# Handing out the scatter of the edges in ones and twos per step, and the rest beside the first layer norm

## What is computed

```
edge_index = stack([src, dst])
x = x + L0_gnn(layernorm(x), src, dst, edge_weight)     # segment_sum(w * x[dst], src), then a projection
x = x + L0_ffn(layernorm(x))                            # 16 experts, 2 per token
x = x + L1_gnn(layernorm(x), src, dst, edge_weight)
x = x + L1_ffn(layernorm(x))
x = x + L2_gnn(layernorm(x), src, dst)                  # graph attention, two layers
x = x + L2_ffn(layernorm(x))
x = x + L3_gnn(layernorm(x), edge_index, edge_weight)   # three rounds of segment sums
x = x + L3_ffn(layernorm(x))
```

## Time and profile before

| | |
|---|---|
| median of 3 runs | 6410.36 us |
| lowest, highest | 6409.36, 6415.48 us |
| span of the profiled execution (its own time; the page gives none around it) | 7555.1 us |
| PE busy in it | 5066.7 us, 67% |
| DVE busy | 2842.8 us, 38% |
| POOL busy | 2221.8 us, 29% |
| bin table's columns (L382) | 392, 402.3 us busy, mean 1026 ns |

### The profile page before, as it was taken

One profiled execution on the slowest core, in us unless ns is written; L12 is line 12 of the kernel. 1 busy time (PEld: TensorE's weight loads), 2 busy tenths in 40 slices (PEclk: granted clock), 3 DMA queues, 4 the chain that ended last, 5 costly groups with the idle time before them and its releaser, 6 DMA issues. The chain is left out here.

```text
span 7555.1 us, 86117 instructions
## 1 busy us (share of the span) xinstructions
PE 5066.7 (67%) x21628; PEld 3356.8 (44%) x21677; DVE 2842.8 (38%) x6162; ACT 1117.7 (15%) x2691; POOL 2221.8 (29%) x2417
## 2 busy tenths in 40 slices
PE   3511969659783597755454965554877969898954
PEld 2410547314771256733222843222767844444433
DVE  4260679201323004244445944445943220202052
ACT  2210235000220002210000120000123220101020
POOL 3356010540244401425553215553300410000014
PEclk9999999769796697977776976777988989999966
DMA  0000023223561223637774827675721644243323
GB/s 14 1 1 1 1 93 139 81 66 120 160 199 65 77 90 123 195 122 228 219 218 137 273 86 224 216 222 160 254 67 40 191 153 153 101 139 115 115 69 114
DMA packets 484296, 952.76 MB, mean 126 GB/s; under 512 B 112617, under 2 KB 292436, under 8 KB 481686
## 3 DMA queue, kind: packets, MB, share of 16 engines
q1 hardware_dynamic: 324614, 633.98, 24.9%
q0 software_dynamic: 114208, 281.05, 12.8%
q10 hardware_dynamic: 45296, 35.56, 1.6%
HBM read 733.91 MB, written 216.46 MB: 126 GB/s over the span
## 5 line engine op out<-in xcount | busy, mean ns | idle before, releaser
L1173 PE MATMUL banks<-ring,xn 128*128 128x512 f32 (+1 forms) x3500 | 1443.9, 568 | 397.6 <-issue 276.9
L1173 PEld LDWEIGHTS banks<-ring,xn 128*128 128x128 f32 x3500 | 644.2, 195 | 1198.0 <-issue 1181.4
L1909 PE MATMUL banks<-agg,hotT 128*128 x1664 | 687.0, 519 | 633.6 <-issue 623.9
L1000 POOL DMA_INDIRECT rows<-pairs,idxr x832 | 804.7, 967 | 640.5 <-DVE scores L1888 373.2
L1909 PEld LDWEIGHTS banks<-agg,hotT 128*128 128x128 f32 x1664 | 319.7, 237 | 949.2 <-issue 945.1
L382 POOL DMA_INDIRECT dst_table<-nodes_pay,nodes_row x392 | 380.0, 969 | 817.5 <-DVEq L1147 478.9
L382 POOL DMA_INDIRECT bin_table<-bins_pay,bins_row x392 | 402.3, 1026 | 592.1 <-ACTq L783 206.8
L1882 DVE TENSOR_TENSOR prod<-banks,rows 128x512 f32<-128x512 f32 x416 | 267.9, 686 | 811.3 <-PE banks L1909 640.7
L1643 PE MATMUL banks<-second,hT 128*128 x1544 | 391.6, 393 | 45.4 <-DVE yr L1689 19.3
L1628 PE MATMUL banks<-xT,w1r 128*128 128x128 f32 x3088 | 403.1, 283 | 12.3 <-DVE xT L1681 7.1
L2162 PE MATMUL banks<-msg,hot 128*128 128x264 f32 x1664 | 384.3, 392 | 16.7 <-DVE msg L2132 16.2
(11 more groups left out here) (355 smaller groups left out, 6931.4 us busy)
## 6 DMA issues: line engine op xcount, KB each, us to landing
ring<-adjacency SPq DMA_DIRECT2D x145, 1280.0 KB
spill<-rows SPq DMA_DIRECT2D x208, 512.0 KB
rows<-spill SPq DMA_DIRECT2D x208, 512.0 KB
w1r<-in_L_ffn_W SPq DMA_DIRECT2D x114, 512.0 KB
adjacency<-strips SPq DMA_DIRECT2D x13, 3200.0 KB
w1r<-in_L_ffn_w SPq DMA_DIRECT2D x65, 512.0 KB
rows<-home_rows SPq DMA_DIRECT2D x35, 640.0 KB
ring<-adjacency SPq DMA_DIRECT2D x25, 640.0 KB
```

Source lines behind the costliest of these rows:

```text
L1000: nc.gpsimd.indirect_dma_start(rows[:, row, :], None, table, bass.IndirectOffsetOnAxis(ap=idxr[:, at + g:at + g + 1], axis=0))\
L1173: last = nc.tensor.matmul(K.ps[2 * (g % 2) + o][:, 0:wd], x[:, t * D + o * P:t * D + (o + 1) * P], ring.buffer[:, n % R, 0:wd // cols, q * ...
L1909: last = nc.tensor.matmul(K.ps[2 + 2 * (jj % 2) + g // 2][:, g % 2 * D:(g % 2 + 1) * D], hotT[:, jj % 2, g * P:(g + 1) * P], tile_of(q, t) ...
```

## The change

The portions beside the two rankings are replaced by a portion per step. GpSimd waits for the stage's own semaphore, `counted`, `evened` or `reduced`, and sends one or two columns each time it has moved on.

```
+    def paced(self, pool, passed, marks, count, ready=None):
+        for m in marks:
+            pool.wait_ge(passed, m)
+            self.columns(pool, count, ready)
...
-                    beside(0, pool, None)
+                    beside(0, pool, counted, None)
...
-                    beside(1, pool, None)
+                    beside(1, pool, evened, None)
...
-                    beside(2, pool, ready)
+                    beside(2, pool, reduced, ready)
...
-SHARES = (120, 38, 36, 156, 12, 6, 11)
+SHARES = (12, 6, 11)
...
-    def beside_bins(part, pool, ready):
+    def beside_bins(part, pool, passed, ready):
         if part == 2:
-            scatter.columns(pool, SHARES[0], ready)
-
-    def beside_nodes(part, pool, ready):
-        scatter.columns(pool, SHARES[1 + part])
+            scatter.paced(pool, passed, range(1, UNITS + 1), 2, ready)
+
+    def beside_nodes(part, pool, passed, ready):
+        scatter.paced(pool, passed, (range(2, 40, 2), range(1, 11), range(1, UNITS + 1))[part], (1, 2, 2)[part])
```

More of the change, by code:

```diff
@@ L974, in place_edges @@
         rank(nc, K, digits, of_node.low, of_node.high, HIGH, chunks, nodes.row[:, :], CHUNKS, beside_nodes)
-        number_pieces(nc, K, pieces.ends, lambda pool: scatter.columns(pool, SHARES[4]))
-        number_chunks(nc, K, chunks.ends, lambda pool: scatter.columns(pool, SHARES[5]))
+        number_pieces(nc, K, pieces.ends, lambda pool: scatter.columns(pool, SHARES[0]))
+        number_chunks(nc, K, chunks.ends, lambda pool: scatter.columns(pool, SHARES[1]))
 def gather_rows(nc, pool, edges, table, rows, idxr, gathered, staged, passed, used, spilled, per):
@@ L2536, in build @@
         K.x, K.xn, K.agg = (st.sb(n, [P, NT * D]) for n in ("x", "xn", "agg"))
-        load_nodes(nc, K, A["x"], lambda pool: of_bins.columns(pool, SHARES[6]))
+        load_nodes(nc, K, A["x"], lambda pool: of_bins.columns(pool, SHARES[2]))
         layer_norm(nc, K, K.x, K.xn, beside=of_bins.finish)
```

## The result

| | before | changed |
|---|---|---|
| median | 6412.92 us (4 runs) | 6583.77 us (4 runs, 6580.10 to 6589.67) |
| span of the profiled execution | 7555.1 us | 6582.9 us |

The changed kernel is slower: the ratio is 1.0269, with a 95% interval of 1.0256 to 1.0281. That is 171 us where I had forecast 146, and 6 us above the end of my range. The direction was right, the size was not. Its profile is 972 us *shorter* than that of before, though the runs are longer.

A forecast was written before the change was run, and what follows sets the result against it. It took the last ranking stages to be bound by TensorE, ScalarE and VectorE taking turns (164.5 and 210.4 us), columns covered. 6410.4 + 142.1 (layer norm) + 2.8 + 1 (waits) = 6556 us; range 6515 to 6578.

The forecast's parts named there:

- The hinge: Whole kernel: the other engines' stalls behind GpSimd's column bursts, together 1130 us, belong to the recorded execution; timed ones have next to none.
- Rival 1: Ranking stages: the stalls behind bursts are the kernel's own and pacing ends them, giving 6205 us, or 6380 with half left; chance 8%.
- Rival 2: Ranking stages: part of the stalls is real and gain and cost cancel, within 13 us of 6410; chance 2%.
- rival 4: First layer norm: a column is cheaper when nothing is recorded, 128 x 0.97 = 124 us, total 6517; chance 4%.
- Rival 5: Rankings: pairs of columns lag behind the steps and end late, 8 us at 1.7 us a column; chance within the port rival's.
- The rankings: Both rankings: fewer columns gain nothing in a timed run, up to 351 us in the recorded execution.
- all 350 columns are already covered: Ranking stages before the change: other engines' work outlasts GpSimd's columns, so the scatter costs nothing there.
- The layer norm: First layer norm: 128 columns instead of 13 make the stage GpSimd's alone, 165.8 us instead of 23.7, +142.1 us.
- The port rival: First layer norm: GpSimd is held up by the port or by landings, up to 10 us more, 6566; chance 8%.
- new waits on GpSimd: Ranking stages: the last pair of columns ends late, +2.8 us for the two last stages, +1 for the middle one.
- my bound of 8 us: Ranking stages: upper bound for the waits on GpSimd together, the lower being 0.

## Why the prediction was right and wrong

**The hinge held.** "The timed executions have next to none of this holding back" was an inference from one sum, 1130 us of stalls against 1145 to be explained. The second recording of the same kernel shows it directly: its span is 6408.8 us, and the same execution was timed at 6410.59. Rival 1 is refuted by it. To this rival the Trainium skill (Runtime: NRT & Kernel Launch, "The ~15µs preamble/postamble breakdown") pointed, which has a profile's total some 6 us above the execution's reported time. No later recording bears the figure out: the span lies 1.7 to 2.1 us below the time of that same execution. Of the first recording the execution's own time isn't on record, only those of others, so the 1145 us neither bear out nor break the page's rule; they say that the recorded execution wasn't like the timed ones. Rival 2 falls with rival 1, and rival 4 too: a column costs 1.277 us in the long layer norm as well, (812.73 - 650.55) / 127, and the recorded execution, 6584.68 us, stands amid the other three. Rival 5 asked for slow columns; in both last parts they took 0.97 us on the mean (95.26 and 95.11 us for 98).

**The rankings gained nothing to speak of**, as said: with bursts of 98 instead of 120 and 156 columns the last stages are 162.7 and 208.2 us instead of 166.0 and 206.1. But "all 350 columns are already covered" was not quite true. Of the 120 the last ended 1.0 us behind VectorE, and their closing of 2.2 us wasn't in the account.

**The layer norm** was the main term, 142.1 us forecast. It measured 168.4 - 20.0 = 148.4. The stage after was forecast at 165.8 and came out at 168.4: behind the last column 4.3 us pass, 2.7 of them the closing, where I had allowed 1.5 for landing and barrier together. The stage before was read from a recording in which stages beside columns were stretched, and that I had just shown to be unfit as a length: 23.7 instead of 20.0. I corrected the rankings for it and not this one.

**The port rival fell.** The normalising stream now ran wholly beside columns, 25 instructions in 8.17 us, and the columns kept to 0.97 us (124.39 / 128). For this instruction the rule of the Trainium skill (SBUF — State Buffer, "SBUF: two separate sides") has no effect here; beside the stream at L633 one column took 14.03 us in the second recording too.

**The step that failed is "new waits on GpSimd"**: 2.8 us for the two last stages and 1 us for the middle one. Measured against the second recording: 175.5 - 166.0 = 9.5, 217.3 - 206.1 = 11.2 and 87.9 - 85.5 = 2.4 us, together 23.1 instead of 3.8. The mechanism was named rightly for the last stages, the last pair starts when VectorE is done and the stage waits for it, but two parts of it were missing. The last two reductions come together, so four columns are late and not two (GpSimd's last column ends 4.1 and 3.3 us behind VectorE's last instruction, where I had let the whole stage end 1.4 us late). That stood in my own row: 931.51 is marked x2. And a stage doesn't end with GpSimd's last column, but after a closing of 8.1 us. In the middle stage it is another case: the steps come so late and so close that GpSimd sends its 20 columns without a pause, ends 0.7 us behind VectorE and closes in 2.0 us. I had no row under my bound of 8 us for all of it. No stage of the recorded kernel ends with a long portion, so no gap in its views shows the closing. Yet its trace holds the drains: GpSimd's ends 1.7 us behind the last of 12 columns, 3.0 and 3.2 behind 36 and 38, 5.2 behind 156. That it grows with the columns could have been read there, though not that it is 8.1 us behind 98.

The sum with the measured terms is 148.4 + 23.1 = 171.5 us, against 170.9 between the medians. With the measured waits the forecast would have been 6556 - 3.8 + 23.1 = 6575 us, and with the layer norm's measured 148.4 us instead of 142.1 it would have been 6582.

## What to carry to other kernels

Compare a profile's span with the timed runs before reading any gap in it. If they differ, find stages that run the same code with and without the suspected neighbour, and subtract; a remedy for a stall that only one recorded execution has costs its full price and returns nothing. Work on a side queue is free until it becomes the last thing in its stage; when handing it out step by step, let it end some steps early, and count what the queue does behind its last instruction, not only the instruction.

## What the runs showed of the hardware

- Behind the indirect transfers of the bin table GpSimd's drain, and with it the barrier, takes the longer the more columns it has sent in the stage, about 0.08 us for each: 2.5 us behind 30, 8.1 behind 98, 9.2 behind 112. Between 112 and 120 it starts anew: 2.2 us behind 120, 3.7 behind 140, 5.1 behind 156. It isn't the landing, which was over 1.1 us behind the last of the 98. A drain every 16 columns, in pauses of GpSimd, brought the last closing to 1.7 us.
- One recorded execution of the kernel before was 1146 us longer than the same program in its next recording, with TensorE held to one matmul every 2.80 us during a burst and the other engines waiting with it. None of the nine recordings since, the changed kernel's and eight others', shows it. What brought it about wasn't tried and stays open.
- The ranking's last parts took 161.7 and 205.4 us at a granted clock of 0.51 to 0.52, about the lower level of 1.2 GHz, and 162.7 and 205.9 us at 1.00. Their length doesn't follow TensorE's clock as it is recorded.
